# A graph-network kernel whose five engine orders are written out by hand: the same steps in a new order

## The chip, the cores and the metric

The kernel runs on one core of a Trainium2 chip, in one launch. The metric is the device time of an execution in microseconds (us). Five engines work side by side, each through its own queue of instructions in order: TensorE (PE, matrix products and transposes), VectorE (DVE), ScalarE (ACT), GpSimd (POOL), and SyncE (SP), which here only issues DMAs. They meet at semaphores alone.

## The reference

Inputs: `x` of 16 batches x 512 nodes x 256 features, one adjacency matrix of 512 x 512 for all batches, and weights. All in fp32. Cut to what matters:

```python
def heads(x, adj, W, a):                 # W: [H,F,O]
    Wh = einsum('bnf,hfo->bhno', x, W)
    e = (Wh @ a[:, :O])[..., :, None] + (Wh @ a[:, O:])[..., None, :]
    e = where(e > 0, e, 0.01 * e)
    e = where(adj > 0, e, -1e9)
    return softmax(e, -1) @ Wh
h = relu(layernorm(x))
h = elu(heads(h, adj, W_heads, a_heads))          # 4 heads of 256, side by side: 1024
out = elu(heads(h, adj, W_out, a_out))            # one head, 1024 -> 256
y = relu(out @ w1 + b1) @ w2 + b2 + out
x = x + layernorm(y) * gamma + beta
h = relu(layernorm(x))                            # second layer, a graph convolution
x = x + deg * (h @ Wi.T + b) + adj @ (h @ Wj.T)
```

## The kernel before, in words

The 16 batches pass one after another through the same steps. Nodes lie on the partitions, in 4 chunks of 128. Products that need fp32 accuracy are made of a high and a low part: ACT copies the high part out of PSUM (`prob_hi`, `whx_hi`, `hx_hi`), and DVE, in one case POOL, subtracts it from the source for the low part (`_lo`); PE multiplies hi x hi, lo x hi and hi x lo (`product`, L747).

The steps of one batch, by engine:

- `load` (SP), `norm_in` (DVE statistics, a small power on POOL, `norm_in_out` on ACT), `turn_in` (PE transposes; hi and lo by ACT and DVE).
- `m1` (h, p), 8 of them: the products of head h with half p of the nodes. DVE's `m1` also copies the two attention columns (`fcol`). `f2send` and `f2bcast` (SP) write one column to DRAM and spread it over all partitions (`f2bc`).
- Attention in units. A unit is half the rows of a head: units 0 to 3 are heads 0 and 1, units 4 and 5 the output head ("BACK") of the batch before, units 6 to 9 heads 2 and 3. A unit's steps: `rowmax` (DVE, two passes of 128x512 over `f2bc` and `mask`, both in SBUF, L625), `rowmath` (DVE, two tiny passes, L633 and L636), `args` (ACT, leaky ReLU and exp), `rinv` and `scale` (DVE, L647, L653), `turn_p` (PE, 8 transposes, L780), `probs` (ACT hi, DVE lo), `attend` (PE, 24 products), `elu_neg`, `elu_exp` (ACT), `elu_out` (DVE, L661), `hx` (ACT hi, L474), `hx_lo` (POOL, L378).
- `mix2` 0 to 3 (PE, 24 products each): the product with `W_out`; the units 4 and 5 follow from it.
- `turn_out`, `ffn1`, `ffn2` (PE), `add_b2` (POOL, L385), `norm_ff`, `gamma` (POOL, L395), `x_beta` (POOL, L390: `x` + beta, after `load_back` has brought `x` again into `xb`), `x2` (DVE).
- `norm_gc`, `turn_gc`, `conv_in` 0 and 1, `conv` (PE), an addition on DVE, `store` (SP). There is one `xb`: the `load_back` of a batch waits for the `store` of the one before.

The order of work is given by five tables at the top of the file, one for each engine. An entry (step, info, late) says: in turn t this engine does the step for batch t - late, if there is such a batch (`run_all`). So each engine runs through its table once a turn, and the batches stand in it at different stages. `late` counts from each engine's own turn 0; only the order in an engine and the semaphores count. At the start and at the end the table's steps for batches that don't exist are left out.

PSUM is four pairs of banks. A program walks PE's table and gives each step that writes PSUM the pair that was taken longest ago; PE waits (`take`) until that pair's last reader is through: for `attend` that is DVE's `elu_out`, for `turn_p` DVE's `probs`, for `m1` DVE's `m1`, for `conv_in` DVE's `conv_in`. So a change of PE's order changes which step waits for which. `arg` has three buffers for units, `prob` and `elu` two.

Within DVE's first `probs` stands `setup_back`, which prepares the weights of the output head.

Of the kernel before, what the change touches and what calls it, by code (L numbers as in the profile page):

```python
# [20 lines left out]
ACT_STEPS = [
    ("probs", 4, 3), ("norm_ff_out", 0, 4), ("elu_neg", 3, 2), ("hx", 2, 2), ("elu_exp", 3, 2), ("probs", 5, 3),
    ("m1", (1, 0), 1), ("args", 7, 2), ("probs", 6, 2), ("elu_neg", 4, 3), ("hx", 3, 2), ("elu_exp", 4, 3), ("args", 8, 2),
    ("elu_neg", 5, 3), ("m1", (1, 1), 1), ("probs", 7, 2), ("elu_exp", 5, 3), ("args", 9, 2), ("elu_neg", 6, 2),
    ("elu_exp", 6, 2), ("probs", 8, 2), ("m1", (2, 0), 1), ("elu_neg", 7, 2), ("hx", 6, 2), ("m1", (2, 1), 1),
    ("elu_exp", 7, 2), ("hx", 7, 2), ("probs", 9, 2), ("elu_neg", 8, 2), ("elu_exp", 8, 2), ("turn_out", 0, 3), ("hx", 8, 2),
    ("elu_neg", 9, 2), ("m1", (3, 0), 1), ("elu_exp", 9, 2), ("hx", 9, 2), ("norm_in_out", 0, 0), ("args", 0, 1),
    ("mix2", 0, 2), ("args", 1, 1), ("mix2", 1, 2), ("norm_gc_out", 0, 4), ("m1", (3, 1), 1), ("probs", 0, 1),
    ("turn_in", 0, 0), ("args", 2, 1), ("turn_gc", 0, 4), ("ffn1", 0, 3), ("probs", 1, 1), ("args", 3, 1), ("elu_neg", 0, 1),
    ("elu_exp", 0, 1), ("conv_in", 0, 4), ("conv_in", 1, 4), ("probs", 2, 1), ("hx", 0, 1), ("m1", (0, 0), 0),  # L30
    ("elu_neg", 1, 1), ("probs", 3, 1), ("elu_exp", 1, 1), ("args", 4, 2), ("args", 5, 2), ("elu_neg", 2, 1), ("hx", 1, 1),
    ("elu_exp", 2, 1), ("m1", (0, 1), 0), ("args", 6, 1),
]
# [869 lines left out]
```

## Time and profile before

| | |
|---|---|
| three runs | 1504.39, 1505.46, 1506.13 us; median 1505.46 |
| the profiled execution | 1505.55 us, its span 1503.5 us |
| mean granted PE clock over the span | 0.982 |
| PE / DVE / ACT / POOL busy | 1339.4 / 1190.4 / 1083.5 / 349.2 us |

The profile covers one execution. Busy time is the time in which an engine's unit worked; matmuls are pipelined and their ends are modelled, so one matmul's duration is longer than the distance to the next. In a timeline row the first number is the start, the second the duration, both in us from the span's start; in brackets stands the engine's idle time before it and what ended it. An operation that is held in the engine by something else shows a longer duration, not idle time.

### The profile page before, as it was taken

How to read it: one execution, taken by the hardware profiler on the slowest of the kernel's cores; microseconds unless marked ns; L12 is line 12 of the kernel's file. 1: busy time of each engine (PE TensorE's matmuls, PEld its weight loads, DVE VectorE, ACT ScalarE, POOL GpSimd, SP SyncE). 2: the span in 40 equal slices, each digit the busy share in tenths (PEclk: the TensorE clock that was granted, in tenths of full speed). 3: DMA queues.
4: the chain of work that ended last, by engine and by line, in shares of the span. 5: the costliest groups of instructions: out<-in, count | busy, mean ns of one | idle time of the engine just before them, and what ended most of it. 6: DMA issues, size and time to landing. Idle time of an engine off the chain costs nothing.

```text
span 1503.5 us, 27090 instructions
## 1 busy us (share of the span) xinstructions
PE 1339.4 (89%) x9944; PEld 1260.0 (84%) x9944; DVE 1190.4 (79%) x2833; ACT 1083.5 (72%) x2037; POOL 349.2 (23%) x234
## 2 busy tenths in 40 slices
PE   1679898999999999999999999999999999998873
PEld 1579898888999888899988888898898999888753
DVE  6687879797988979797887979789797978968442
ACT  1577978787868778777877877687787778678431
POOL 0012123232231322223131223213122321403121
PEclk9889999999999999999999999999999999999996
DMA  4101111111101111110111111001121101101001
...
DMA packets 53091, 54.07 MB, mean 36 GB/s; under 512 B 14048, under 2 KB 41696, under 8 KB 52832
## 3 DMA queue, kind: packets, MB, share of 16 engines
...
## 4 chain that ended last, share of the span: by engine, by line
PE 51%; DVE 35%; issue 6%; ACT 5%; POOL 2%; DMA 2%; POOLq 0%; ACTq 0%; DVEq 0%; SPq 0%
PE ps L747 33%; DVE arg L625 12%; PE ps L780 5%; DVE prob_lo L606 4%; DVE arg L653 4%; PE ps L830 4%; PE ps L871 4%; PE ps L840 3%; DVE elu L661 2%; DVE zneg L633 2%; DVE whx_lo L606 2%; DVE st L587 1%; POOL hx_lo L378 1%; DVE xb L699 1%; PE ps L849 1%
## 5 line engine op out<-in xcount | busy, mean ns | idle before, releaser
L378 POOL TENSOR_TENSOR hx_lo<-elu,hx_hi 128x512 fp32r<-128x512 f32 x128 | 171.2, 1338 | 622.7 <-ACT hx_hi L474 622.7
L747 PE MATMUL ps<-prob_hi,whx_hi 128*128 128x256 f32 x1024 | 298.5, 291 | 11.4 <-DVE wk L661 7.6
L747 PE MATMUL ps<-prob_lo,whx_hi 128*128 128x256 f32 x1024 | 289.7, 283 | 0.0
L747 PE MATMUL ps<-prob_hi,whx_lo 128*128 128x256 f32 x1024 | 289.2, 282 | 0.0
L625 DVE CUSTOM_DVE_ANT_0 arg<-f2bc,mask 128x512 f32<-128x512 f32 x320 | 278.7, 907 | 1.9 <-DMA f2bc<-f_rows 1.6
L444 ACT ACTIVATE arg<-arg,nmax 128x512 f32<-128x512 f32 x320 | 227.7, 718 | 0.6 <-DVE nmax L636 0.5
L440 ACT ACTIVATE arg<-arg,fcol 128x512 f32<-128x512 f32 x320 | 213.5, 721 | 12.1 <-DVE gmax L625 12.1
L780 PE MATMUL ps<-ident,arg 128*128 128x128 f32 x1280 | 186.9, 290 | 36.9 <-DVE arg L653 32.4
L747 PEld LDWEIGHTS ps<-prob_hi,whx_hi 128*128 128x128 f32 x1024 | 196.1, 192 | 17.2 <-issue 9.7
L780 PEld LDWEIGHTS ps<-ident,arg 128*128 128x128 f32 x1280 | 170.6, 209 | 45.0 <-DVE arg L653 34.8
L450 ACT ACTIVATE prob_hi<-ps 128x1024 fp32r<-128x1024 f32 x160 | 163.4, 1021 | 58.7 <-PE ps L747 33.1
L606 DVE TENSOR_TENSOR prob_lo<-ps,prob_hi 128x1024 fp32r<-128x1024 f32 x160 | 194.7, 1217 | 12.5 <-ACT prob_hi L450 9.8
L747 PEld LDWEIGHTS ps<-prob_hi,whx_lo 128*128 128x128 f32 x1024 | 195.6, 191 | 0.4
L747 PEld LDWEIGHTS ps<-prob_lo,whx_hi 128*128 128x128 f32 x1024 | 195.5, 191 | 0.0
L747 PE MATMUL ps<-wo_hi,hx_hi 128*128 128x258 f32 x512 | 146.0, 285 | 22.9 <-POOL hx_lo L378 22.9
L653 DVE TENSOR_SCALAR arg<-arg,rinv 128x512 f32<-128x512 f32 x320 | 153.5, 521 | 1.9
L747 PE MATMUL ps<-wh_hi,hT_hi 128*128 128x258 f32 x512 | 150.9, 295 | 2.4 <-DVE hT_lo L606 2.4
L747 PE MATMUL ps<-wh_lo,hT_hi 128*128 128x258 f32 x512 | 145.8, 285 | 0.0
L747 PE MATMUL ps<-wh_hi,hT_lo 128*128 128x258 f32 x512 | 145.4, 284 | 0.0
L747 PE MATMUL ps<-wo_lo,hx_hi 128*128 128x258 f32 x512 | 144.4, 282 | 0.0
L747 PE MATMUL ps<-wo_hi,hx_lo 128*128 128x258 f32 x512 | 143.8, 281 | 0.0
L433 ACT ACTIVATE whx_hi<-ps 128x512 fp32r<-128x512 f32 x128 | 75.8, 592 | 88.5 <-PE ps L747 88.5
...
## 6 DMA issues: line engine op xcount, KB each, us to landing
...
f_rows<-fcol SPq DMA_DIRECT2D x80, 2.0 KB, 3.4
...
```

The lines of the kernel that those rows point to most:

```text
L378: pool.tensor_tensor(out=hx[1][:, 2 * c.h:2 * c.h + 2, c.u * HN:(c.u + 1) * HN], in0=elu[:, c.buf, :, :], in1=hx[0][:, 2 * c.h:2 * c.h + 2 ...
L433: act.activation(whx[:, 2 * p:2 * p + 2, h, 0:F], pairs[c.pair][:, :, 0:F], ACT.Copy).then_inc(m1_hi, 1)
L440: act.activation(a[:, n, :], a[:, n, :], ACT.Prelu, bias=f1[:, n:n + 1], alpha=SLOPE).then_inc(arg_lin, 1)
L444: i = act.activation(a[:, n, :], a[:, n, :], ACT.Exp, bias=nmax[:, c.abuf, n:n + 1], accum_out=rsum[:, c.abuf, n:n + 1])
L450: act.activation(prob[0][:, c.buf, :, :].rearrange("p j i -> p (j i)"), pairs[c.pair][:, :, :].rearrange("p a n -> p (a n)"), ACT.Copy).th ...
L606: return dve.tensor_tensor(out=dst, in0=src, in1=hi.bitcast(fp32), op=ALU.subtract)
L625: dve.tensor_tensor_reduce(out=arg[:, c.abuf, n, :], in0=f2bc[:, head % F2S, :], in1=mask[:, 2 * c.u + n, :], scale=1.0, scalar=-3.0e38, o ...
L653: i = dve.tensor_scalar(arg[:, c.abuf, n, :], arg[:, c.abuf, n, :], rinv[:, c.abuf, n:n + 1], None, ALU.mult)
L747: i = pe.matmul(out, a, b_, start=(k == 0), stop=(k == n - 1))
L780: i = pe.transpose(p[:, j, n, :], arg[:, c.abuf, n, :].rearrange("p (q c) -> p c q", c=NC)[:, j, :], ident[:, :])
L830: i = pe.matmul(pairs[c.pair][:, o, :], w1_sb[:, k, o * P:(o + 1) * P], outT[:, k, :], start=(k == 0), stop=(k == KC - 1))
L871: i = pe.matmul(pairs[c.pair][:, n // 2, (n % 2) * F:(n % 2 + 1) * F], adjT[:, j, n * P:(n + 1) * P], mj, start=(j == 0 and s == 0), stop= ...
```

## The change

The five tables have new orders. The entries are the same; `late` is counted from other turns, and where an entry moved past the end of a turn, it serves another batch. `setup_back` uses `wk[:, 3, :]` in place of `elu[:, 0, 0, :]` for an intermediate row. The new order was made by a planner that takes it that a DVE pass over SBUF alone and a large POOL operation never run at the same time. Nothing else differs. The old tables of ACT and DVE, the same entries in another order, are left out of the diff here.

```diff
@@ -5,52 +5,52 @@
 SP_STEPS = [
-    ("f2send", -1, 3), ("load", 0, 0), ("f2send", 2, 2), ("f2bcast", -1, 3), ("f2send", 3, 2), ("f2bcast", 2, 2),
-    ("store", 0, 5), ("f2bcast", 3, 2), ("f2send", 0, 1), ("load_back", 0, 4), ("f2send", 1, 1), ("f2bcast", 0, 1),
+    ("f2send", -1, 3), ("f2send", 2, 2), ("f2bcast", -1, 3), ("f2send", 3, 2), ("load", 0, 0), ("f2bcast", 2, 2),
+    ("store", 0, 5), ("f2bcast", 3, 2), ("load_back", 0, 4), ("f2send", 0, 1), ("f2send", 1, 1), ("f2bcast", 0, 1),
     ("f2bcast", 1, 1),
 ]
 PE_STEPS = [
-    ("m1", (1, 1), 1), ("attend", 5, 3), ("turn_p", 7, 2), ("attend", 6, 2), ("turn_p", 8, 2), ("m1", (2, 0), 1),
-    ("attend", 7, 2), ("m1", (2, 1), 1), ("turn_p", 9, 2), ("attend", 8, 2), ("turn_out", 0, 3), ("m1", (3, 0), 1),
-    ("attend", 9, 2), ("mix2", 0, 2), ("mix2", 1, 2), ("mix2", 2, 2), ("mix2", 3, 2), ("m1", (3, 1), 1), ("turn_p", 0, 1),
-    ("turn_in", 0, 0), ("ffn1", 0, 3), ("turn_gc", 0, 4), ("turn_p", 1, 1), ("attend", 0, 1), ("conv_in", 0, 4),
-    ("conv_in", 1, 4), ("turn_p", 2, 1), ("m1", (0, 0), 0), ("attend", 1, 1), ("turn_p", 3, 1), ("ffn2", 0, 3),
-    ("attend", 2, 1), ("m1", (0, 1), 0), ("conv", 0, 4), ("turn_p", 4, 2), ("attend", 3, 1), ("turn_p", 5, 2),
-    ("m1", (1, 0), 0), ("turn_p", 6, 1), ("attend", 4, 2),
+    ("attend", 6, 3), ("turn_out", 0, 4), ("turn_p", 8, 3), ("attend", 7, 3), ("turn_p", 9, 3), ("m1", (2, 0), 2),
+    ("attend", 8, 3), ("attend", 9, 3), ("ffn1", 0, 4), ("turn_gc", 0, 5), ("m1", (2, 1), 2), ("mix2", 0, 3), ("mix2", 1, 3),
+    ("mix2", 2, 3), ("mix2", 3, 3), ("m1", (3, 0), 2), ("turn_p", 0, 2), ("turn_p", 1, 2), ("conv_in", 0, 5),
+    ("m1", (3, 1), 2), ("turn_in", 0, 1), ("conv_in", 1, 5), ("attend", 0, 2), ("turn_p", 2, 2), ("ffn2", 0, 4),
+    ("attend", 1, 2), ("turn_p", 3, 2), ("m1", (0, 0), 1), ("conv", 0, 5), ("attend", 2, 2), ("turn_p", 4, 3),
+    ("m1", (0, 1), 1), ("attend", 3, 2), ("turn_p", 5, 3), ("m1", (1, 0), 1), ("attend", 4, 3), ("turn_p", 6, 2),
+    ("m1", (1, 1), 1), ("attend", 5, 3), ("turn_p", 7, 2),
 ]
 ACT_STEPS = [
...
+    ("elu_neg", 6, 3), ("elu_exp", 6, 3), ("turn_out", 0, 4), ("probs", 8, 3), ("hx", 6, 3), ("elu_neg", 7, 3),
+    ("probs", 9, 3), ("elu_exp", 7, 3), ("hx", 7, 3), ("m1", (2, 0), 2), ("elu_neg", 8, 3), ("elu_exp", 8, 3), ("hx", 8, 3),
+    ("norm_gc_out", 0, 5), ("elu_neg", 9, 3), ("elu_exp", 9, 3), ("norm_in_out", 0, 1), ("hx", 9, 3), ("turn_gc", 0, 5),
+    ("m1", (2, 1), 2), ("ffn1", 0, 4), ("args", 0, 2), ("args", 1, 2), ("mix2", 0, 3), ("args", 2, 2), ("mix2", 1, 3),
+    ("m1", (3, 0), 2), ("probs", 0, 2), ("probs", 1, 2), ("args", 3, 2), ("m1", (3, 1), 2), ("conv_in", 0, 5),
+    ("turn_in", 0, 1), ("conv_in", 1, 5), ("elu_neg", 0, 2), ("elu_exp", 0, 2), ("probs", 2, 2), ("args", 4, 3),
+    ("hx", 0, 2), ("args", 5, 3), ("elu_neg", 1, 2), ("elu_exp", 1, 2), ("probs", 3, 2), ("m1", (0, 0), 1), ("hx", 1, 2),
+    ("args", 6, 2), ("elu_neg", 2, 2), ("norm_ff_out", 0, 4), ("elu_exp", 2, 2), ("probs", 4, 3), ("m1", (0, 1), 1),
+    ("args", 7, 2), ("hx", 2, 2), ("elu_neg", 3, 2), ("elu_exp", 3, 2), ("probs", 5, 3), ("m1", (1, 0), 1), ("hx", 3, 2),
+    ("probs", 6, 2), ("elu_neg", 4, 3), ("elu_exp", 4, 3), ("m1", (1, 1), 1), ("args", 8, 2), ("elu_neg", 5, 3),
+    ("elu_exp", 5, 3), ("probs", 7, 2), ("args", 9, 2),
 ]
 DVE_STEPS = [
...
+    ("scale", 5, 7), ("rowmax", 7, 6), ("rowmath", 7, 6), ("elu_out", 2, 6), ("rinv", 6, 6), ("probs", 4, 7),
+    ("m1", (0, 1), 5), ("rowmax", 8, 6), ("scale", 6, 6), ("rinv", 7, 6), ("elu_out", 3, 6), ("probs", 5, 7),
+    ("m1", (1, 0), 5), ("rowmath", 8, 6), ("x2", 0, 8), ("scale", 7, 6), ("elu_out", 4, 7), ("probs", 6, 6),
+    ("m1", (1, 1), 5), ("rowmax", 9, 6), ("rinv", 8, 6), ("elu_out", 5, 7), ("rowmath", 9, 6), ("scale", 8, 6),
+    ("probs", 7, 6), ("rinv", 9, 6), ("scale", 9, 6), ("elu_out", 6, 6), ("probs", 8, 6), ("norm_gc", 0, 8), ("probs", 9, 6),
+    ("elu_out", 7, 6), ("norm_gc_out", 0, 8), ("norm_in", 0, 4), ("elu_out", 8, 6), ("norm_in_out", 0, 4), ("m1", (2, 0), 5),
+    ("elu_out", 9, 6), ("rowmax", 0, 5), ("rowmath", 0, 5), ("rowmax", 1, 5), ("rinv", 0, 5), ("rowmath", 1, 5),
+    ("rowmax", 2, 5), ("scale", 0, 5), ("turn_gc", 0, 8), ("m1", (2, 1), 5), ("rowmath", 2, 5), ("mix2", 0, 6),
+    ("rinv", 1, 5), ("scale", 1, 5), ("mix2", 1, 6), ("rowmax", 3, 5), ("rowmath", 3, 5), ("m1", (3, 0), 5), ("probs", 0, 5),
+    ("rinv", 2, 5), ("probs", 1, 5), ("conv_in", 0, 8), ("scale", 2, 5), ("m1", (3, 1), 5), ("turn_in", 0, 4),
+    ("conv_in", 1, 8), ("rowmax", 4, 6), ("rinv", 3, 5), ("elu_out", 0, 5), ("rowmath", 4, 6), ("rowmax", 5, 6),
+    ("rowmath", 5, 6), ("scale", 3, 5), ("ffn2", 0, 7), ("rinv", 4, 6), ("probs", 2, 5), ("scale", 4, 6), ("rowmax", 6, 5),
+    ("elu_out", 1, 5), ("rowmath", 6, 5), ("norm_ff", 0, 7), ("conv", 0, 8), ("rinv", 5, 6), ("probs", 3, 5),
+    ("norm_ff_out", 0, 7), ("m1", (0, 0), 4),
 ]
 POOL_STEPS = [
-    ("hx_lo", 7, 4), ("hx_lo", 8, 4), ("norm_gc", 0, 6), ("add_b2", 0, 5), ("hx_lo", 9, 4), ("norm_in", 0, 1),
     ("hx_lo", 0, 3), ("hx_lo", 1, 3), ("norm_ff", 0, 5), ("gamma", 0, 5), ("hx_lo", 2, 3), ("x_beta", 0, 5), ("hx_lo", 3, 3),
-    ("hx_lo", 6, 3),
+    ("hx_lo", 6, 3), ("norm_gc", 0, 5), ("hx_lo", 7, 3), ("norm_in", 0, 1), ("hx_lo", 8, 3), ("hx_lo", 9, 3),
+    ("add_b2", 0, 4),
 ]
@@ -564,7 +564,7 @@
 
             def setup_back():
                 dve.wait_ge(ld[LD_BG], 16)
-                part = elu[:, 0, 0, :]
+                part = wk[:, 3, :]
                 link(dve.tensor_copy(w2x[:, 0, :], wk[:, 2, :]))
                 link(dve.tensor_tensor(out=part, in0=wk[:, 2, :], in1=w2x[:, 0, :].bitcast(fp32), op=ALU.subtract))
                 link(dve.tensor_scalar(part, part, ident[:, 1:2], None, ALU.mult))
```

## Rows read from the trace of the kernel before

**Rows 1.** The page: busy time and share of an engine; the chain's shares by engine.

```profile
PE 1339.4 (89%) x9944; PEld 1260.0 (84%) x9944; DVE 1190.4 (79%) x2833; ACT 1083.5 (72%) x2037; POOL 349.2 (23%) x234
...
PE 51%; DVE 35%; issue 6%; ACT 5%; POOL 2%; DMA 2%; POOLq 0%; ACTq 0%; DVEq 0%; SPq 0%
```

**Rows 2.** Windows: stretch, its length, busy time of each engine (instructions), PE clock, DMA.

```profile
0.00:135.00 135.00, 79.34 (x579) 77.09 (x580) 97.13 (x273) 70.86 (x128) 15.86 (x21) 0.94 0.22 69
135.00:1360.00 1225.00, 1158.06 (x8752) 1095.03 (x8751) 1025.24 (x2415) 956.13 (x1811) 301.31 (x194) 1.00 0.13 33
317.60:1273.50 955.90, 905.02 (x6822) 854.90 (x6822) 801.01 (x1872) 738.95 (x1397) 239.95 (x153) 1.00 0.13 34
1360.00:1503.50 143.50, 102.03 (x618) 87.84 (x617) 68.06 (x146) 56.48 (x100) 32.00 (x19) 0.87 0.10 28
```

**Rows 3.** Waits of PE: who <- whom: us in total, times, longest.

```profile
PE ps L780 <- DVE arg L653: 32.4, 11, 10.6
PE ps L747 <- POOL hx_lo L378: 22.9, 14, 2.0
PE ps L747 <- DVE elu L661: 18.2, 14, 1.4
```

**Rows 4.** Timeline of all engines, 703 to 709.5 us: start, duration, engine, line.

```profile
703.01 0.63 ACT L469 ACTIVATE elu<-elu 128x512 f32<-128x512 f32 x1
...
703.11 2.44 POOL L385 TENSOR_TENSOR wk<-wk,b_bc 128x1024 f32<-128x1024 f32 x1
...
703.23 2.87 DVE L625 CUSTOM_DVE_ANT_0 arg<-f2bc,mask 128x512 f32<-128x512 f32 x1
...
706.64 0.68 DVE L661 SCALAR_TENSOR_TENSOR elu<-elu,ps 128x512 f32<-128x512 f32 x1
...
709.38 0.39 PE L747 MATMUL ps<-wo_hi,hx_hi 128*128 128x258 f32 x1 [1.65 <-POOL hx_lo L378]
```

**Rows 5.** The same view, 669 to 674 us.

```profile
669.25 2.53 POOL L395 TENSOR_TENSOR wk<-wk,gamma_bc 128x1024 f32<-128x1024 f32 x1 [5.11 <-ACT wk L418]
669.44 1.22 DVE L606 TENSOR_TENSOR prob_lo<-ps,prob_hi 128x1024 fp32r<-128x1024 f32 x1
...
670.58 1.22 DVE L633 SCALAR_TENSOR_TENSOR zneg<-fcol,gmax 128x2 f32<-128x2 f32 x1
...
671.84 1.20 DVE L636 SCALAR_TENSOR_TENSOR nmax<-zneg 128x2 f32<-128x2 f32 x1
...
673.78 0.36 PE L747 MATMUL ps<-w2x_hi,prob_hi 128*128 128x256 f32 x1 [1.35 <-DVE elu L661]
```

**Rows 6.** Groups by line and form: busy us, mean ns of one | idle before.

```profile
L625 DVE CUSTOM_DVE_ANT_0 arg<-f2bc,mask 128x512 f32<-128x512 f32 x320 | 278.7, 907 | 1.9 <-DMA f2bc<-f_rows 1.6 <-issue 0.3
...
L633 DVE SCALAR_TENSOR_TENSOR zneg<-fcol,gmax 128x2 f32<-128x2 f32 x160 | 48.8, 305 | 2.3
```

**Rows 7.** Three lines of the kernel: durations in ns, least/median/longest.

```profile
L625 DVE CUSTOM_DVE_ANT_0 arg<-f2bc,mask x320: 674/685/2899, 55.7 to 1419.3; 128x512 f32<-128x512 f32 x160
...
L587 DVE BATCH_NORM_STATS2 st<-wk x64: 407/411/428, 228.8 to 1461.5; 128x6 f32<-128x256 f32 x64
...
L378 POOL TENSOR_TENSOR hx_lo<-elu,hx_hi x128: 1262/1292/1678, 85.2 to 1393.5; 128x512 fp32r<-128x512 f32 x128
```

**Rows 8.** The chain in order of time, within one turn: start, us, what.

```profile
686.91 4.33 PE ps L747 x36
...
718.64 3.44 PE ps L830 x8
```

**Rows 9.** The same view, of the start and the end of the span.

```profile
80.66 1.98 PE ps L780 x8
...
1401.93 3.43 PE ps L830 x8
...
1464.35 2.91 DMA out_x<-xb
1467.32 3.79 DMA xb<-in_x
```

More of the change, by code:

```diff
@@ L20 @@
+    ("m1", (3, 1), 2), ("turn_in", 0, 1), ("conv_in", 1, 5), ("attend", 0, 2), ("turn_p", 2, 2), ("ffn2", 0, 4),
+    ("attend", 1, 2), ("turn_p", 3, 2), ("m1", (0, 0), 1), ("conv", 0, 5), ("attend", 2, 2), ("turn_p", 4, 3),
+    ("m1", (0, 1), 1), ("attend", 3, 2), ("turn_p", 5, 3), ("m1", (1, 0), 1), ("attend", 4, 3), ("turn_p", 6, 2),
+    ("m1", (1, 1), 1), ("attend", 5, 3), ("turn_p", 7, 2),
 ]
 ACT_STEPS = [
-    ("probs", 4, 3), ("norm_ff_out", 0, 4), ("elu_neg", 3, 2), ("hx", 2, 2), ("elu_exp", 3, 2), ("probs", 5, 3),
@@ L23 @@
[L23 to L32, printed above, removed]
+    ("elu_neg", 6, 3), ("elu_exp", 6, 3), ("turn_out", 0, 4), ("probs", 8, 3), ("hx", 6, 3), ("elu_neg", 7, 3),
@@ L33 @@
 ]
 DVE_STEPS = [
-    ("m1", (1, 1), 3), ("elu_out", 5, 5), ("probs", 7, 4), ("rinv", 9, 4), ("scale", 9, 4), ("elu_out", 6, 4),
-    ("probs", 8, 4), ("m1", (2, 0), 3), ("elu_out", 7, 4), ("m1", (2, 1), 3), ("rowmax", 0, 3), ("probs", 9, 4),
-    ("elu_out", 8, 4), ("rowmath", 0, 3), ("norm_gc", 0, 6), ("rowmax", 1, 3), ("rowmath", 1, 3), ("rowmax", 2, 3),
-    ("elu_out", 9, 4), ("rowmath", 2, 3), ("m1", (3, 0), 3), ("mix2", 0, 4), ("rinv", 0, 3), ("scale", 0, 3), ("rinv", 1, 3),
-    ("norm_gc_out", 0, 6), ("scale", 1, 3), ("mix2", 1, 4), ("m1", (3, 1), 3), ("probs", 0, 3), ("rowmax", 3, 3),
@@ L40 @@
-    ("turn_in", 0, 2), ("rinv", 2, 3), ("rowmath", 3, 3), ("turn_gc", 0, 6), ("scale", 2, 3), ("probs", 1, 3),
-    ("norm_in", 0, 1), ("conv_in", 0, 6), ("rinv", 3, 3), ("elu_out", 0, 3), ("scale", 3, 3), ("conv_in", 1, 6),
-    ("probs", 2, 3), ("rowmax", 4, 4), ("rowmath", 4, 4), ("m1", (0, 0), 2), ("rowmax", 5, 4), ("rowmath", 5, 4),
-    ("probs", 3, 3), ("elu_out", 1, 3), ("rowmax", 6, 3), ("ffn2", 0, 5), ("rinv", 4, 4), ("rowmath", 6, 3),
-    ("norm_ff", 0, 5), ("scale", 4, 4), ("rinv", 5, 4), ("elu_out", 2, 3), ("m1", (0, 1), 2), ("conv", 0, 6),
@@ L45 @@
-    ("norm_ff_out", 0, 5), ("scale", 5, 4), ("rowmax", 7, 3), ("rinv", 6, 3), ("norm_in_out", 0, 1), ("scale", 6, 3),
-    ("probs", 4, 4), ("rowmath", 7, 3), ("elu_out", 3, 3), ("probs", 5, 4), ("rowmax", 8, 3), ("m1", (1, 0), 2),
-    ("rinv", 7, 3), ("rowmath", 8, 3), ("scale", 7, 3), ("probs", 6, 3), ("x2", 0, 5), ("elu_out", 4, 4), ("rowmax", 9, 3),
-    ("rowmath", 9, 3), ("rinv", 8, 3), ("scale", 8, 3),
+    ("scale", 5, 7), ("rowmax", 7, 6), ("rowmath", 7, 6), ("elu_out", 2, 6), ("rinv", 6, 6), ("probs", 4, 7),
```

## The prediction, on record before the change was run

> **What bounds the kernel now.** I read the page first [rows 1]: TensorE (PE) is busy 1339.4 of 1503.5 us, and its tenths in the 40 slices are nines between a thin start and a thin end. Yet the chain that ended last runs for 35% through DVE. So PE is the engine with the most work, and DVE is what PE waits for.
>
> The windows [rows 2] cut that in three. From 135 to 1360 us the kernel is in its steady part: 1225.0 us with 1158.1 of PE, idle 66.9. Before it PE is idle 135.0 - 79.3 = 55.7, behind it 143.5 - 102.0 = 41.5. Eleven turns of the steps (one for each batch) take 955.9 us with 905.0 of PE: 86.9 us a turn, 82.3 of it work. The floor of a turn is thus about 82 us, and a turn stands 4.6 us above it.
>
> PE's waits [rows 3] name who is late: `hx_lo` of POOL (22.9 us, 14 times, once a turn), and DVE's `elu` (18.2, 14 times). The 32.4 us on `arg` are 11 waits only, up to 10.6 us long: they lie at the start and the end.
>
> The timeline shows why DVE is late. At 703.11 POOL begins add_b2 (2.44 us); DVE's rowmax, 0.68 us when undisturbed, begins at 703.23 and lasts 2.87 us, until POOL has ended. Behind it in DVE's queue stands elu_out of unit 9, ready since ACT's exp ended near 703.6; it starts at 706.64, then hx 707.35, hx_lo 708.06, and PE starts mix2 (2) at 709.38 after 1.65 us of waiting [rows 4]. The second wait is the same: POOL's gamma at 669.25 and the hx_lo behind it hold two DVE operations on 2 elements a row (zneg 1.22 us, nmax 1.20, where 0.16 is usual); elu_out follows only when they are through, and attend 4, which needs the PSUM pair of attend 3, starts at 673.78, 1.35 late [rows 5]. A prob_lo pass at 669.44, which reads PSUM, took its usual 1.22 us in the middle of gamma. So passes whose operands are all in SBUF wait for a large POOL operation to end, passes that read PSUM don't. Over the run rowmax pays 320 x (0.907 - 0.685) = 71 us and zneg 160 x (0.305 - 0.16) = 23 us [rows 6, 7]; nmax and scale are held likewise, and it comes to some 8 us of DVE a turn. Nearly all of PE's steady idle time hangs on it. Not every pass over SBUF is held: the batch-norm passes, with one tensor read, last 0.43 us at most at a median of 0.41 [rows 7].
>
> **The change part by part.** No instruction is added or removed: the same steps stand in another order on five engines, and five small passes of setup_back write into `wk` in place of `elu`. These are the same passes on the same sizes, run once, and I take them at nothing.
>
> PE's order. From the chain [rows 8]: 36 matmuls take 4.33 us, 0.12 each, so an attend or a mix2 (24) takes 2.9, an m1 (12) 1.45; a turn_p starts 0.9 before what follows it; ffn1 takes 3.44, ffn2 3.3, conv 3.85, conv_in 3.0, the transposes 0.9. What matters is how much PE work lies between a step and the one that waits for its result:
> - attend 9 to mix2 (2), the wait of rows 4: before, mix2 0 and 1, 5.8 us. After, ffn1, turn_gc, m1 (2,1) come first: 3.4 + 0.9 + 1.45 + 5.8 = 11.6. The chain between took 7.4 us (attend 9 ended at 702.0) with the hold in it and needs some 4.6 without. The 1.65 us go either way.
> - attend 3 to the step that takes its PSUM pair, the wait of rows 5: before it was attend 4, with turn_p 5, m1 (1,0), turn_p 6 between, 3.3 us. After, attend 4 takes the pair of m1 (0,1), and attend 3's goes to turn_p 6, with turn_p 5, m1 (1,0), attend 4 between: 5.3 us. The release needs ACT 0.60 + 0.63 and DVE 0.68, about 2.0 with the hand-overs: 3.3 us are left for queueing, more than one hold of 2.5 us.
> - The tightest such distances after: attend 5 to turn_p 8 (turn_p 7, attend 6, turn_out: 4.6), attend 6 to turn_p 9 (4.6), mix2 (3) to conv_in (0) (m1, two turn_p: 3.3). The last has a short release: one ACT copy of 0.58 and one DVE pass with its copy of f, 0.8.
>
> DVE and POOL. A turn has about 65 us of DVE work undisturbed (801.0 / 11 = 72.8 less the 8 held) and 239.95 / 11 = 21.8 of POOL [rows 2]. In the new DVE table I laid the passes beside PE's steps with the durations above. The densest place is around conv: conv (PE) ends, DVE adds (1.2), probs 3 (1.2), norm_ff_out, m1 (0,0) (0.75), and their PSUM pairs are wanted by turn_p 4 and m1 (0,1) within 2.9 and 3.8 us of conv's end: room of 0.3 us each. Then norm_ff_out on ACT (2.0) stands between elu_neg 2 and elu_exp 2, and probs 4, elu_out 3, probs 5 come 0.1 to 1.2 us before they are due. POOL's gamma, hx_lo 2 and x_beta fall into this stretch, against rowmax 7, rowmax 8 and scale 6. So I expect small waits to stay here: between 0 (the room holds) and 2.5 us (one hold in full) a turn. I take 0.9, nearer the lower end, since each hold meets some of the room. The rest of the turn, from attend 6 to ffn2, has 1 to 8 us of room at every step; add_b2 now runs behind hx_lo 9, against rowmax 0 and 1, after which DVE waits for ACT's args 0 anyway.
>
> POOL can be the one that is held: hx_lo has a median of 1.29 us and a longest time of 1.68 [rows 7]. The Trainium skill (SBUF — State Buffer, "Who interferes with whom") puts it generally: issue order, not the operation's shape, decides who blocks, for the whole instruction. By that rule hx_lo 2 and x_beta, which here follow each other on a chain with 1 us of room (below), could each stand behind a whole rowmax pass of 0.69 us: 1.4 us against a room of 1.0, and the sum would be 14 x 0.4 = 6 us higher, 1464. The trace agrees in kind and shows the smaller size, 0.39 us at most; the 0.9 above is worked out without the rule.
>
> Steady part: of 66.9 us of idle, about 6 belong to waits of the filling pipeline (turn_p 4 of the first batches, 3.4 and 2.3 at their longest), which stay. 60.9 go, 14 turns x 0.9 = 12.6 come back: -48.3 us. The ends of the range from this step: nothing comes back (-61), or 2.5 a turn (-26).
>
> SP's queue. load moves behind two f2send, and load_back before f2send 0. The load has more than 40 us before its norm_in; but f2bcast 2 stands behind load and f2send 3, and f2send 3 waits for DVE's m1 (3,1). In the first turn that read now comes behind setup_back instead of before it: up to 2 us late for rowmax 6. In steady state the row is there some 8 us before rowmax 6. Cost 0 to 2, taken 1.
>
> Start. setup_back holds DVE from 66.5 to 77.1 us and turn_p 2 starts at 80.66 [rows 9]. In the new table rowmax 3, rowmath 3 come before probs 0 (+1.4), while rowmax 3 and turn_in no longer stand between setup_back and scale 2, but probs 1 does: 77.1 + 1.4 + 0.1 + 1.2 + 0.8 = 80.6. No change; bounds -3 and +3, since each engine's order there differs in several places.
>
> End. The last batch is a chain that the change leaves as it was: store, load, x_beta (2.91 + 3.79 us and POOL's 2.34), norms, turn_gc, conv_in, conv: 39 us from 1464.35 to 1503.5 [rows 9]. Ahead of it, the end of mix2 (3), 1401.93 [rows 9], to turn_p 4, 1424.45, took 22.5 us, as ffn1, turn_gc, conv_in, ffn2, conv stood between. Now ffn1 and turn_gc (4.3) run before mix2 and the wait behind it shrinks to about 16 + 4; but ACT's norm_ff_out comes before probs 4 now (+2). Sum about 0; bounds -3 and +3.
>
> Sum against the profiled execution: 1505.55 (span 1503.5 and 2.05 around it) - 48.3 + 1 = 1458 us. That execution and the median of the runs, 1505.46, differ by 0.1 us, so it holds for both.
>
> **The rivals.**
> *Half the gain.* The order has its passes just in time, and a hold that falls elsewhere than planned pushes the next: 2 to 3 us a turn are left. For it: the room of 0.1 to 0.3 us around conv, and that POOL starts when ACT or a DMA releases it, not by a plan. Against: the 5.3 us distances. 1505.5 - 61 + 14 x 2.5 + 1 = 1480 us.
> *The holds move and cost as much.* POOL's 22 us and DVE's two-operand passes are what they were; if the new meetings delay passes with no room, 4.3 us a turn stay: 1505 us. Against: the distance that made the largest wait has doubled.
> *Slower.* One chain turns into the bound: conv's end, DVE 1.2, store, load, then in POOL's queue hx_lo 2 and only then x_beta, x2, scale 7, elu_out 4, with turn_p 7 due 18.7 us after conv's end. Without a wait for hx_lo 2 it is 1.2 + 9.0 + 1.2 + 0.8 + 0.6 = 12.8 us; hx 2 stands late in ACT's queue and I get 17.7, 1 us early. Before, x2 ended 16.3 us after conv (665.2 to 681.5), and I get the same for it now. If hx_lo 2 came 5.9 us later than I have it, a turn would be 82.0 + 4.9, the 86.9 of now; each further us costs 14. At one us beyond: 1520 us.
>
> **How the numbers follow.** Forecast 0.67 (1444 to 1467), half the gain 0.19, moved 0.04, slower 0.10. A measurement here tells a change of over 0.2%, about 3 us: the runs spread 1504.4 to 1506.1. Faster by more: 0.67 + 0.19 + 0.01 = 0.87; within: 0.03; slower: 0.10. The range takes in the forecast with its ends and most of the half gain: 1444 to 1482.
>
> **What would show it.** Right: windows of one turn of 82.5 to 83.5 us; no wait of mix2 for `hx_lo`; the mean of rowmax and zneg nearer 0.69 and 0.16, or still high with PE not waiting (then the distances did it, and not the avoided meetings). Step by step: turn_p 2 at 79 to 82 us in the first turn; 39 us from the last conv but one to the end. Wrong: PE's waits around conv, on `prob_lo`, `fcol` or `elu`, of more than 2 us a turn, or x_beta ending close to turn_p 7.

## The result and the profile after

| | before | after |
|---|---|---|
| median (spread) | 1505.8 us (1504.4 to 1509.4, 4 runs) | 1429.67 us (1428.93 to 1431.62, 4 runs) |
| profiled execution, span | 1505.55, 1503.5 us | 1429.68, 1427.6 us |
| PE / DVE / ACT / POOL busy | 1339.4 / 1190.4 / 1083.5 / 349.2 us | 1328.0 / 1106.9 / 1091.9 / 344.9 us |

The ratio after to before is 0.9493, 95% interval 0.9474 to 0.9512: 76 us faster, 28 us more than forecast and below the range.

The page after, to be laid beside [rows 1]: busy times, and the chain's shares by engine.

```profile
PE 1328.0 (93%) x9944; PEld 1259.2 (88%) x9944; DVE 1106.9 (78%) x2833; ACT 1091.9 (76%) x2037; POOL 344.9 (24%) x234
...
PE 86%; DVE 7%; ACT 3%; issue 2%; DMA 1%; POOL 0%; POOLq 0%; SPq 0%; ACTq 0%; DVEq 0%
```

The chain now runs through PE: DVE's share fell from 35% to 7%. DVE does the same passes in 83.5 us less of busy time. The windows, as in [rows 2]:

```profile
0.00:135.00 135.00, 81.09 (x576) 78.49 (x576) 94.69 (x273) 73.34 (x134) 15.03 (x21) 0.84 0.22 69
135.00:1276.00 1141.00, 1134.70 (x8666) 1082.20 (x8664) 938.12 (x2389) 952.76 (x1788) 295.92 (x192) 1.00 0.14 35
303.69:1197.75 894.06, 894.06 (x6822) 852.98 (x6821) 735.38 (x1882) 744.66 (x1398) 237.97 (x154) 1.00 0.14 36
1276.00:1427.60 151.60, 112.23 (x708) 98.49 (x706) 74.08 (x173) 65.76 (x117) 33.91 (x21) 0.88 0.10 28
```

In the third row, eleven turns, PE has no shown idle time at all: 81.28 us a turn, against 86.90. Where the 75.9 us came from: idle time of PE over the span fell from 164.1 to 99.6 us (-64.5), and its busy time, for the same 9944 matmuls, from 1339.4 to 1328.0 (-11.4). By place: the conv of batch 0 starts at 303.7 in place of 313.6 us (-9.9), the eleven turns behind it give -61.9, what follows -4.1.

PE's waits, longest first, as in [rows 3]. `hx_lo` is gone; the waits that are left lie at the start and the end.

```profile
PE ps L780 <- DVE arg L653: 24.1, 7, 8.4
PE ps L849 <- ACT ff L418: 17.5, 1, 17.5
PE ps L758 <- ACT xin L418: 16.8, 1, 16.8
PE ps L716 <- DVE mask L520: 10.7, 1, 10.7
...
PE ps L747 <- DVE prob_lo L606: 4.9, 6, 2.2
```

The groups and the durations of one line, as in [rows 6, 7]:

```profile
L625 DVE CUSTOM_DVE_ANT_0 arg<-f2bc,mask 128x512 f32<-128x512 f32 x320 | 228.7, 751 | 33.6 <-PE ps L780 29.9 <-DMA f2bc<-f_rows 2.9 <-issue 0.6
...
L633 DVE SCALAR_TENSOR_TENSOR zneg<-fcol,gmax 128x2 f32<-128x2 f32 x160 | 40.5, 253 | 2.3
```

```profile
L625 DVE CUSTOM_DVE_ANT_0 arg<-f2bc,mask x320: 674/687/2914, 56.9 to 1340.4; 128x512 f32<-128x512 f32 x160
L653 DVE TENSOR_SCALAR arg<-arg,rinv x320: 473/480/1526, 62.8 to 1347.2; 128x512 f32<-128x512 f32 x160
L390 POOL TENSOR_TENSOR xb<-xb,beta_bc x16: 2337/2582/2845, 235.0 to 1395.3; 128x1024 f32<-128x1024 f32 x16
```

By the means of a pass, rowmax pays 320 x (0.751 - 0.687) = 20 us where it paid 71, zneg 160 x (0.253 - 0.16) = 15 where it paid 23: the holds of rowmax went for the most part, those of zneg did not. The place where they remain is the one around conv. The timeline there, ACT's rows and most of PE's left out:

```profile
805.86 1.92 DVE L653 TENSOR_SCALAR arg<-arg,rinv 128x512 f32<-128x512 f32 x2
...
805.98 1.51 POOL L378 TENSOR_TENSOR hx_lo<-elu,hx_hi 128x512 fp32r<-128x512 f32 x1 [2.65 <-ACT hx_hi L474]
...
807.45 2.59 POOL L390 TENSOR_TENSOR xb<-xb,beta_bc 128x1024 f32<-128x1024 f32 x1
...
807.77 0.66 DVE L661 SCALAR_TENSOR_TENSOR elu<-elu,ps 128x512 f32<-128x512 f32 x1
...
810.16 1.16 DVE L633 SCALAR_TENSOR_TENSOR zneg<-fcol,gmax 128x2 f32<-128x2 f32 x1
...
811.43 1.22 DVE L679 TENSOR_TENSOR xb<-xb,wk 128x1024 f32<-128x1024 f32 x1
...
813.37 0.68 DVE L661 SCALAR_TENSOR_TENSOR wk<-elu,ps 128x512 f32<-128x512 f32 x1
...
814.19 1.20 PE L780 MATMUL ps<-ident,arg 128*128 128x128 f32 x8
```

scale 6 takes 1.92 us in place of 0.87. x_beta begins behind hx_lo 2 and ends at 810.04. x2 starts 1.4 us later: rowmath 8 stands ahead of it in DVE's queue, and hx_lo 3, which runs on POOL from 810.01 to 811.30, holds its zneg. elu_out 4 ends at 814.05, and turn_p 7 starts 0.14 us later. No idle time stands there, but the row of turn_p 7 is 1.20 us long where the other turn_p rows of this stretch have 1.13, and the step behind it starts 1.13 us after it, where without holds (the second run below) it is 0.88.

### The profile page after: what moved, and what is told of

The parts are those of the page before. It is cut to its first block, busy times and chain, and to the rows that moved or that the text cites. A ratio compares the mean times of both kernels' runs of the same rounds, so it can differ in the third digit from the quotient of the medians.

```text
span 1427.6 us, 27090 instructions
## 1 busy us (share of the span) xinstructions
PE 1328.0 (93%) x9944; PEld 1259.2 (88%) x9944; DVE 1106.9 (78%) x2833; ACT 1091.9 (76%) x2037; POOL 344.9 (24%) x234
## 4 chain that ended last, share of the span: by engine, by line
PE 86%; DVE 7%; ACT 3%; issue 2%; DMA 1%; POOL 0%; POOLq 0%; SPq 0%; ACTq 0%; DVEq 0%
PE ps L747 61%; PE ps L780 10%; PE ps L830 4%; PE ps L871 4%; PE ps L840 4%; DVE arg L625 1%; PE ps L849 1%; PE ps L758 1%; PE ps L818 1%; DVE prob_lo L606 1%; ACT arg L444 1%; PE ps L750 1%; ACT prob_hi L450 0%; DMA arg<-in_adj 0%; DVE f2bc L547 0%
## 5 line engine op out<-in xcount | busy, mean ns | idle before, releaser
L625 DVE CUSTOM_DVE_ANT_0 arg<-f2bc,mask 128x512 f32<-128x512 f32 x320 | 228.7, 751 | 33.6 <-PE ps L780 29.9
L780 PE MATMUL ps<-ident,arg 128*128 128x128 f32 x1280 | 182.2, 288 | 27.5 <-DVE arg L653 24.1
L780 PEld LDWEIGHTS ps<-ident,arg 128*128 128x128 f32 x1280 | 167.0, 209 | 30.9 <-DVE arg L653 28.3
L747 PE MATMUL ps<-wh_hi,hT_hi 128*128 128x258 f32 x512 | 153.9, 301 | 2.9 <-DVE hT_lo L606 2.4
L465 ACT ACTIVATE elu<-ps 128x512 f32<-128x512 f32 x160 | 93.9, 587 | 77.3 <-PE ps L747 77.3
```

What stands on the lines that cost most here:

```text
L465: act.activation(elu[:, c.buf, :, :], pairs[c.pair][:, :, 0:F], ACT.Relu, scale=-1.0).then_inc(elu_neg, 1)
L625: dve.tensor_tensor_reduce(out=arg[:, c.abuf, n, :], in0=f2bc[:, head % F2S, :], in1=mask[:, 2 * c.u + n, :], scale=1.0, scalar=-3.0e38, o ...
L747: i = pe.matmul(out, a, b_, start=(k == 0), stop=(k == n - 1))
L780: i = pe.transpose(p[:, j, n, :], arg[:, c.abuf, n, :].rearrange("p (q c) -> p c q", c=NC)[:, j, :], ident[:, :])
```

## The experiments

Ratios are to the kernel before, run on the same chip (1510 to 1515 us there). "A turn" is the distance of the conv steps of batches 0 to 11, divided by 11, from the profile. The first question was what the new order does: spare the meetings, or take the cover of PE work in front of them.

**No holds, old order, and no holds, new order.** In both kernels POOL's hx_lo, add_b2, gamma and x_beta work on 2 columns; the rest of their tiles stays uncomputed.

```diff
-pool.tensor_tensor(out=wk[:, :, :], in0=wk[:, :, :], in1=b2_bc[:, None, :]...
+pool.tensor_tensor(out=wk[:, :, 0:2], in0=wk[:, :, 0:2], in1=b2_bc[:, None, 0:2]...
```

> The order of before, but POOL's four large operations (hx_lo, add_b2, gamma, x_beta) work on 2 of 256 or 512 columns alone; the low part of hx and three additions are left out for the rest (a memset of hx_lo at the start instead). Theory H (the holds of DVE by POOL are the whole steady loss of the old order): no hold is left, a turn falls from 86.9 to about 81.3 us, the time to 1505 - 14 x 5.6 = 1427 us. Rival O (the old order of PE's steps, with its short distances, is what costs, holds or not): a turn stays at 85 us or more, the time at 1480 or more. This also tells what a turn without any wait costs: if 82.0 to 82.3, the old order of PE's steps is itself some 0.8 us a turn longer than the new one; if 81.3, the waits cost more than their idle time shows.

> The order of after with the same four operations shrunk to 2 columns. Theory H: the holds that are left in the new order (64 us of DVE over the run) lie fully under PE's work, so the time stays within 3 us of 1430. Rival: some of PE's steps start 0.15 us behind a semaphore without showing idle time, and a turn falls from 81.3 to about 80.8: 1422 us.

Measured: 1421.0 us, ratio 0.9389 (0.9364 to 0.9414), and 1416.4 us, ratio 0.9356 (0.9327 to 0.9385). The windows of eleven turns, of the old order and of the new one:

```profile
308.12:1196.34 888.22, 888.22 (x6823) 850.50 (x6822) 704.96 (x1873) 737.63 (x1398) 68.97 (x153) 1.00 0.13 37
```

```profile
297.86:1188.41 890.55, 890.55 (x6822) 851.02 (x6821) 703.17 (x1882) 740.67 (x1398) 69.62 (x154) 1.00 0.13 36
```

80.75 us a turn in the old order, 80.96 in the new. So the old order is as good as the new one where POOL's work is small: the whole gain of the steady part is taken from what POOL's large operations cost. They cost the old order 86.90 - 80.75 = 6.15 us a turn, of which the profile showed 4.63 as idle, and cost the new one 0.32. Step by step, a turn of the kernel before with seven waits is 6.59 us longer than one without holds, and 4.94 of it is shown as idle: 1.65 us are not, 0.24 for a wait. The second expectation was missed: the span is 10.8 us below that of the changed kernel, not within 3 us, 2.9 of it ahead of the first conv, 3.5 in the eleven turns, 4.4 behind them; its rival had the turn nearly right.

These two runs take away more than the holds, since POOL's own operations are short as well (hx_lo 0.2 us in place of 1.3). For hx_lo 9 a run below settles that: with 50 memsets ahead of it its result comes 1.0 us later than at its real length (1.78 + 0.53 against 1.29), no rowmax or zneg pass is held, and PE waits 0.07 us a turn. For gamma and x_beta no run separates their own length from the holds; that DVE is held under them is read from the durations.

**One, two and three swaps in the old order.** Only the entries that change places are shown. The third edit turns the order of three entries round.

```diff
-    ("add_b2", 0, 5), ("hx_lo", 9, 4),                     POOL, first swap
+    ("hx_lo", 9, 4), ("add_b2", 0, 5),
-    ("rowmath", 7, 3), ("elu_out", 3, 3),                  DVE, second
+    ("elu_out", 3, 3), ("rowmath", 7, 3),
-    ("rowmath", 8, 3), ("scale", 7, 3), ("probs", 6, 3),   DVE, third
+    ("probs", 6, 3), ("scale", 7, 3), ("rowmath", 8, 3),
```

> The order of before with two entries of POOL's table exchanged: hx_lo 9 before add_b2. Theory H: the hold of rowmax at the end of the turn is gone (add_b2 then runs where DVE waits for ACT anyway), PE's 1.65 us before mix2 (2) go, and what a wait costs beyond its idle time: 1.7 to 2.0 a turn, 14 turns: 1478 to 1482 us. Rival (the hold only moves and strikes another pass, or another wait of the same turn takes its place, since the pair of banks is short there): less than 0.7 a turn, 1496 or more.

> As e3, and in DVE's table elu_out 3 before rowmath 7. Theory H: elu_out 3 no longer stands behind the tiny passes that gamma and hx_lo hold, attend 4 doesn't wait (1.35 us and some 0.1 to 0.3 beside): another 1.4 to 1.7 a turn below e3, 1455 to 1460 us. Rival (the turn is a ring of short distances: the next wait takes the place): e4 equals e3 within 5 us.

> The old order with three swaps of neighbours: add_b2 behind hx_lo 9 (POOL), elu_out 3 ahead of rowmath 7 (DVE), and now probs 6 and scale 7 ahead of rowmath 8 (DVE). In the run with two swaps PE waited 1.48 us a turn at turn_p 7 for prob_lo of unit 6, because rowmath 8, held 2.5 us by x_beta and hx_lo 3, stood ahead of it. Theory (holds delay a pass that PE needs soon; the order decides only what stands behind a held pass): that wait goes, about 1.5 us of 85.05 a turn, so a turn of 83.5 and a total ratio to before of 0.977 - 21/1513 = 0.963. Rival (the next wait takes its place, as it did with the second swap): scale 7 is now the pass that is held, until hx_lo 3 ends, and rowmath 8 comes 0.3 us later for args 8, so that turn_p 7 or turn_p 8 waits instead: ratio 0.973 to 0.979.

Measured: 1484.3 us (ratio 0.9809, 0.9782 to 0.9837), 1478.7 (0.9771, 0.974 to 0.980), 1467.1 (0.9702, 0.9682 to 0.9723); turns of 85.08, 84.95 and 83.37 us. The first swap gave its wait back, as the theory of the holds says. The second gave 0.13 us a turn, 5.6 us in the median: next to nothing, as its rival has it. With two swaps:

```profile
753.71 2.94 POOL L390 TENSOR_TENSOR xb<-xb,beta_bc 128x1024 f32<-128x1024 f32 x1 [1.69 <-DMA xb<-in_x]
...
755.06 1.62 DVE L633 SCALAR_TENSOR_TENSOR zneg<-fcol,gmax 128x2 f32<-128x2 f32 x1
756.60 1.30 POOL L378 TENSOR_TENSOR hx_lo<-elu,hx_hi 128x512 fp32r<-128x512 f32 x1
756.72 1.21 DVE L636 SCALAR_TENSOR_TENSOR nmax<-zneg 128x2 f32<-128x2 f32 x1
...
759.99 1.20 PE L780 MATMUL ps<-ident,arg 128*128 128x128 f32 x8 [1.44 <-DVE prob_lo L606]
...
761.91 0.36 PE L747 MATMUL ps<-prob_hi,whx_hi 128*128 128x256 f32 x1 [0.72 <-DVE wk L661]
```

attend 4 no longer waits, so PE comes earlier to turn_p 7 and waits there for a prob_lo that stands behind two held operations on 2 elements a row. Behind these two waits, of 1.44 and 0.72 us, PE's granted clock is lower. Windows of the same kernel:

```profile
753.00:760.00 7.00, 5.56 (x48) 5.39 (x46) 6.97 (x14) 6.34 (x14) 4.19 (x2) 1.00 0.00 1
761.90:764.50 2.60, 2.58 (x13) 2.60 (x14) 2.50 (x10) 2.35 (x5) 0.00 (x0) 0.58 0.00 0
```

The granted clock is 1.00 ahead of the waits and 0.58 behind them, most of that stretch at its 1.2 GHz level: products that started 120 ns apart start 215 ns apart. Eight of the eleven turns have 13 to 15 such products and take 85.2 to 85.4 us, the three without take 84.1 to 84.3. All eight have this pair of waits; of the three without, one has it too, and two wait 1.7 us at attend 5 instead. So the pair can bring the clock down, and does not always. The third swap won 1.6 us a turn, between its theory (0.963) and its rival (0.973): the wait of turn_p 7 and the slow products are gone, but attend 6 now waits 1.06 us.

**Cover in place of avoidance, old order.** m1 (3,1) goes in front of mix2 0, first on PE alone, then on PE, ACT and DVE.

```diff
-    ("attend", 9, 2), ("mix2", 0, 2), ... ("mix2", 3, 2), ("m1", (3, 1), 1),
+    ("attend", 9, 2), ("m1", (3, 1), 1), ("mix2", 0, 2), ... ("mix2", 3, 2),
```

> The old order, where PE alone is changed: m1 (3,1) is moved from behind mix2 3 to between attend 9 and mix2 0. The hold of rowmax under add_b2 stays; the PE work between attend 9 and mix2 2 grows from 5.8 to 7.3 us. If distance covers a hold as well as its removal does: the wait of mix2 for hx_lo (22.9 us over 14 turns) falls below 3 us, the total falls by what the swap of add_b2 and hx_lo 9 gave (ratio 0.981, at most 0.985). Rival: the hold is not shortened, so DVE stays 2.2 us late and the wait appears at the next step that needs a DVE result (turn_p 0 or conv_in): ratio 0.99 to 1.00.

> The old order; m1 (3,1) moved from behind mix2 3 to ahead of mix2 0 on PE as in the run before (1560.6 us, where turn_in waited 3.2 us a turn for DVE's m1 (3,1)), and now its copy on ACT and its pass on DVE are moved ahead of those of mix2 0 as well. Theory (distance covers a hold): the wait of turn_in is gone, that of mix2 2 for hx_lo (22.9 us over 14 turns) stays below 8 us though rowmax is held by add_b2 as before; ratio to before 0.98 to 0.99. Rival (every table is laid on the others, and a step moved by 8 us meets new due passes wherever it goes): another wait of over 1 us a turn, ratio 1.00 or more.

Measured: 1560.6 us, ratio 1.0325 (1.0303 to 1.0348), slower; and 1505.2 us, ratio 0.9945 (0.9924 to 0.9966). With PE alone moved, neither the theory nor its rival had it slower. One row of its waits:

```profile
PE ps L758 <- DVE fcol L617: 41.2, 14, 3.2
```

turn_in takes the PSUM pair of m1 (3,1) now, and DVE's pass that frees it still stood where it was, behind ACT's norm_gc_out: a step moved on PE without its readers costs more than a hold. With the readers moved too:

```profile
PE ps L747 <- DVE elu L661: 16.5, 12, 1.4
...
PE ps L747 <- DVE hT_lo L606: 6.7, 13, 2.4
PE ps L747 <- POOL hx_lo L378: 4.1, 13, 0.6
```

1.5 us more of cover took `hx_lo` from 22.9 to 4.1 us, so distance does hide a hold. But attend 0 and others came to wait instead, 9 waits a turn where there were 5 or 7, and the total was half a percent less. The expectation of 0.98 to 0.99 was missed, between it and the rival.

**add_b2 early again, new order.**

```diff
-    ("hx_lo", 8, 3), ("hx_lo", 9, 3),
-    ("add_b2", 0, 4),
+    ("hx_lo", 8, 3), ("add_b2", 0, 4), ("hx_lo", 9, 3),
```

> The new order; on POOL alone add_b2 goes back ahead of hx_lo 9, as it stood in the old order. Theory that distance does it (11.6 us of PE work between attend 9 and mix2 2, chain of 4.6 us and one hold of 2.4): mix2 2 does not wait, time within 2 us of the changed kernel's 1429, ratio to before 0.945 to 0.950. Theory that the avoided meeting does it: hx_lo 9 comes 2.4 us later, a wait of 1.5 us a turn comes back, 1450 us, ratio 0.960.

Measured: 1427.9 us, ratio 0.9434 (0.9413 to 0.9455); the changed kernel unaltered, once more but on another chip, had 1429.0 and 0.9454 (0.9435 to 0.9474), where 0.949, give or take 0.003, was expected. No change, as the theory of distance has it, but for a weaker reason: add_b2 ran at 751.2 to 753.5, in a gap of POOL ahead of hx_lo 9 and under no pass of DVE that it holds. It met nothing, so this run does not tell the theories apart. What does bear on it is that hx_lo 9 ends 3.9 us before mix2 2 starts in the changed kernel: more than one whole hold.

**Which POOL operation holds which pass.** Old order; each large POOL operation is a single memset, so the values of these tiles are not computed.

> The old order, where each of POOL's four large operations (hx_lo, add_b2, gamma, x_beta) is one memset of the same tile: it writes and reads nothing. If any large POOL operation holds a DVE pass with two SBUF operands: rowmax, zneg, nmax and scale that start under a memset last until its end, as before. If it takes a POOL operation with two operands read: they keep their usual 0.68, 0.16, 0.16 and 0.24 us, PE has no wait in a turn, and a turn is 80.7 to 81.0 us.

Measured: 1421.0 us, 80.75 us a turn (one run). Durations, least/median/longest, of rowmax, zneg and scale, in that order:

```profile
L629 DVE CUSTOM_DVE_ANT_0 arg<-f2bc,mask x320: 680/686/694, 55.6 to 1337.6; 128x512 f32<-128x512 f32 x160
...
L637 DVE SCALAR_TENSOR_TENSOR zneg<-fcol,gmax x160: 139/155/163, 56.9 to 1338.3; 128x2 f32<-128x2 f32 x160
...
L657 DVE TENSOR_SCALAR arg<-arg,rinv x320: 467/482/1249, 61.3 to 1344.3; 128x512 f32<-128x512 f32 x160
```

43 rowmax and 24 zneg passes began under a memset and none was held; scale still was, up to 1.25 us. So there are two kinds: passes with two SBUF operands are held by a POOL operation that reads, the scale pass by one that only writes as well. The Trainium skill (SBUF — State Buffer, "Who interferes with whom") has these two cases: an instruction with two SBUF inputs meets only a GpSimd instruction that reads SBUF, while `tensor_scalar`, which scale is, can enter a mode that takes both ports and then meets any. This trace agrees with both.

**The other edit alone.** setup_back writes into wk in the old order.

```diff
-                part = elu[:, 0, 0, :]
+                part = wk[:, 3, :]
```

> The old order with the other edit of the change alone: setup_back writes its intermediate row into wk in place of elu. Expected: nothing, within 0.3% of before. Rival: at the start unit 0's elu no longer waits for setup_back, up to 3 us less.

Measured: 1513.0 us (one run) against 1514.4: nothing.

**What a wait costs.** The write-only kernel never waits in a turn; small memsets of a spare tile ahead of hx_lo 9 delay it by a time that the trace shows. They are 30 and 50 of 8 columns, then 130 and 180 of 2.

```diff
+                if (c.h, c.u) == (3, 1):
+                    for k in range(130):
+                        pool.memset(pad[:, k, :], 0.0)
```

> The old order with POOL's four large operations as single memsets (a turn of 80.75 us, no wait), and on POOL ahead of the hx_lo of unit 9 another 30 memsets of 8 columns of a spare tile, some 3 us. PE must wait for hx_lo in mix2 2 once a turn. If a wait costs more than the idle time that is shown (theory): the turn is longer than 80.75 by the shown idle and 0.2 to 0.6 us more. Rival: the turn grows by the shown idle exactly (within 0.05), and the 1.5 us between the busy time of a turn before (82.3) and 80.75 have another reason.

> The same with 50 memsets, some 5 us. Theory: a wait about 2 us longer than with 30, and the part that is not shown is the same (a fixed cost of a wait, not a share of it). Rival: no part that is not shown.

> POOL's large operations as single memsets, and 130 memsets of 2 columns ahead of the hx_lo of unit 9, some 4.7 us. PE waits in mix2 once a turn, 2 to 3 us (with 1.8 us of delay it had just begun to). Theory (a wait costs more than it shows): the turn is 80.7 us plus the shown idle plus 0.1 to 0.6. Rival: 79.9 to 80.7 plus the shown idle and nothing more.

> The same with 180 memsets, some 6.5 us. Both theories: 1.8 us more of shown idle a turn than with 130; the turn grows by the same 1.8 if what is not shown is fixed for one wait, by more if it is a share of it.

Measured: turns of 79.92, 80.70, 83.42 and 85.87 us, with 0.02, 0.07, 2.13 and 3.53 us of shown idle (one run each). The first two delays were 1.1 and 1.8 us long, where 3 and 5 were expected, and covered, so they say nothing on waits. With 130 memsets PE waits once a turn, in mix2 2:

```profile
773.95 0.28 PE L755 MATMUL ps<-wo_lo,hx_hi 128*128 128x258 f32 x1
776.64 0.39 PE L755 MATMUL ps<-wo_hi,hx_hi 128*128 128x258 f32 x1 [2.41 <-POOL hx_lo L383]
776.87 0.28 PE L755 MATMUL ps<-wo_hi,hx_lo 128*128 128x258 f32 x1
...
777.47 0.42 PE L755 MATMUL ps<-wo_hi,hx_hi 128*128 128x258 f32 x1
777.68 0.42 PE L755 MATMUL ps<-wo_hi,hx_lo 128*128 128x258 f32 x1
```

The products start 0.12 us apart, here 2.69 and then 0.23: 2.68 us are lost where 2.41 are shown. Two things hide in it: idle time counts only from the modelled end of the product before (0.28 - 0.12 = 0.16), and the first product after a wait takes 0.11 longer. This wait thus costs 0.27 us more than its idle time. On top, PE's clock falls soon after: five of the eleven turns have 13 to 15 products 215 ns apart and take 84.2 to 84.6 us, the six others 82.65. With 180, all eleven have them, 11 to 25. Windows of a turn with and a turn without, 130 memsets:

```profile
311.57:395.72 84.15, 82.08 (x622) 78.50 (x621) 64.71 (x172) 67.00 (x128) 14.61 (x144) 0.98 0.14 36
395.72:478.37 82.65, 80.58 (x622) 77.00 (x621) 64.28 (x172) 66.99 (x128) 14.61 (x144) 1.00 0.14 36
```

The totals alone do not decide for the theory. The mean turn, 83.42, is 0.59 above 80.7 and its idle time, as it had it, but the part of the clock is in that. The six turns without slow products are 82.65, which less 2.07 of idle is 80.58: the rival's figure. Taken step by step, both things are there. mix2 1 and 2 of such a turn take 2.34 us more than in the write-only kernel, for 2.07 of idle: the 0.27 again. And the attends of this run take up to 0.07 us less each, some 0.45 a turn (the last section has this pace). With 180 memsets 1.40 us of idle a turn came on top, not 1.8, and the turn grew by 2.45, as more turns have slow products. So 0.27 for a wait is shown at the one step, and the 0.24 above agrees; that it is the same for every length is not shown. The part of the clock is a second one; here it came behind waits of 2.07 us and more.

**The last batch.** New order. Batch 15's second x goes into the free first tile by a load of its own, early, and gets beta right behind batch 14's; x2, norms and store of that batch use this tile.

```diff
+                if c.b == B - 2:
+                    wait(sp, h_turned, B)
+                    sp.dma_start(xin[:, :, :], x_v[B - 1]).then_inc(xb_loaded_last, 16)
```

> The new order, where the last batch alone is changed: its second x goes by a load of its own into the tile of the first load, early, and gets beta right behind batch 14's, so that its x2 and norms need not wait for the store of batch 14. In the changed kernel PE is idle 17.5 us ahead of the last turn_gc, of which store 2.9 + load 3.8 + POOL 2.3 are this chain. Expected: that gap falls to about 8 to 13 us, the total by 4 to 9 us against the new order in the same job (ratio to before lower by 0.003 to 0.006). Rival: ffn2 and the norm behind it of the last batch end no earlier than the load does, and nothing changes (within 1 us).

Measured: 1423.5 us (1423.1 to 1424.3), ratio 0.9418 (0.9398 to 0.9437), against 1429.0 for the changed kernel on the same chip: 5.5 us less, as expected. The wait ahead of the last turn_gc:

```profile
PE ps L865 <- ACT ff L434: 12.7, 1, 12.7
```

4.8 us less of it. This is the fastest kernel that computes everything. On it, rowmath 8 was moved:

```diff
-    ("rowmath", 8, 6), ("x2", 0, 8), ("scale", 7, 6), ("elu_out", 4, 7),
+    ("x2", 0, 8), ("scale", 7, 6), ("elu_out", 4, 7), ("rowmath", 8, 6),
```

> The new order with the early load of the last batch, and on DVE rowmath 8 moved from ahead of x2 to behind elu_out 4: it stood 1.3 us there under POOL's hx_lo 3, ahead of elu_out 4, for whose pair turn_p 7 has 0.15 us of room. Expected, if the last 0.3 us a turn come from the holds before elu_out 4: 81.0 us a turn, 4 us less in all than with the early load alone (1419 against 1423.5). Rival: args 8 on ACT is then due later than ACT reaches it, and probs 7 or turn_p 8 waits: 1424 to 1430.

Measured: 1426.0 us, 81.42 us a turn against 81.27: not faster, and 2.5 us slower in the median (on another chip, ratio 0.9445, 0.9433 to 0.9458), as the rival has it. PE comes to wait 0.05 us a turn, for prob_lo.

## Why the prediction was right in direction and 28 us off

What bounds the kernel: right. PE waited for DVE, DVE for POOL, and with the holds gone the chain is PE's.

Idle time that goes: 60.9 us were to go from the steady part and 6 to stay; of 66.9 there are 1141.0 - 1134.7 = 6.3 left. Right.

Distances. mix2 2 does not wait, with 3.9 us to spare where 11.6 - 7.4 = 4.2 were worked out with a hold in the chain, and 7.0 without. That it comes near is luck: no rowmax pass stood in the chain now, but elu_neg 9 and hx 9 wait on ACT behind norm_gc_out and norm_in_out (2.06 us each), and the chain took 7.4 us again in place of 4.6. Around conv the plan had 0.3 us of room for turn_p 4 and m1 (0,1); measured, 0.27 and 0.41 lie between the last release and the start. These rooms were right, and the conclusion from them was not. Avoided meetings or distance: of the 94 us of holds on rowmax and zneg 35 are left, and none of them shows as idle time in the turns; no run divides the gain between the two.

"Small waits stay here ... I take 0.9": this is the first term that failed, 12.6 us. No idle time comes back; by the run without holds the meetings cost 0.32 us a turn, 4.5 in fourteen, and that lies in busy time. The holds do meet this stretch (scale 6 at 1.92 us, zneg 8 at 1.16), and the chain hx_lo 2, x_beta, x2, elu_out 4 reaches turn_p 7 with 0.14 us left, but the program repeats to 0.03 us from turn to turn (81.26 to 81.29), so here a room of 0.2 us was nearly as good as one of 2. I had priced it as if the meetings scattered.

"The floor of a turn is thus about 82 us": the second, 11.4 us. It was read off PE's busy time, and busy time holds the hidden part of each wait. The turns before had 6.5 waits each; by 0.24 to 0.27 that is 1.6 to 1.75 us, and without holds the busy time of the same order is 82.27 - 80.75 = 1.5 less. I had taken the busy time of a turn as the same before and after, without a reason. The sum of before had to be 6.15 us a turn and was 4.6. PE's clock has no part in it: 1.00 in both steady windows, and none of the products of 256 columns at 215 ns. A turn was to take 82.5 to 83.5 us and takes 81.28. Without this term the prediction's own bounds do not reach the result: with nothing coming back, SP at no cost, and the start and the end each 3 us better, they give about 1439 (the stated range ended at 1444 even so), and the floor had no bounds.

These two make 24.0 of 28.6; the rest is 3.9 us less idle time at the two ends and the 1 us for SP's queue, which PE did not pay, less the 0.3 by which more idle stayed than the 6. SP: rowmax waited 2.9 us in all for its row, in two waits, in place of 1.6. Start: turn_p 2 at 81.99 (79 to 82 foretold). The rest of what I called the start, up to conv 0, holds about two turns with waits, and so gave 9.9. End: -4.1, beyond the bound of 3; the last batch's store, load and norms are as they were:

```profile
1388.39 2.91 DMA out_x<-xb
1391.36 3.90 DMA xb<-in_x
```

The rule of the Trainium skill that issue order decides who is held (SBUF — State Buffer, "Who interferes with whom"): POOL was held too, hx_lo 2 for 0.2 us (1.51) and x_beta for 0.25 (a median of 2.58 against its least, 2.34), not 0.7 each; add_b2, for 0.55 (2.89 against 2.34), most of a rowmax pass. The rule read as a whole pass for each of the first two gave 6 us more; the trace has smaller holds there, and no shown wait came of them.

Rivals. Half the gain: no. The holds move and cost as much: true of the second swap in the old order, not of this order, where all entries moved together. Slower by way of x_beta: no, but its chain used up all it had. From conv's end (795.35) x2 ended after 17.3 us where 16.3 were worked out, and elu_out 4 after 18.7 where I had 17.7, just as turn_p 7 falls due. The last link was not x_beta, which had ended 1.4 us before x2 began, but rowmath 8 under hx_lo 3. This is where the new order would break first.
